# Attention with four score tiles in a row and a group's values in one run: eight weight slots, half of the scalings on GpSimd, four heads of Wo split early

## The chip, the cores and the metric

One core of one Trainium2 chip. The metric is the device time of one execution in microseconds, the median of the runs shown.

## What is computed

The kernel computes a chain of four residual layers on x (64 sequences, 32 tokens, 512 wide). The first, the one that the change touches, is attention with a paged cache:

```python
q, k, v = x @ Wq.T, x @ Wk.T, x @ Wv.T          # 32 query heads, 8 key heads, 128 wide
q, k = rope(rmsnorm(q)), rope(rmsnorm(k))
kc, vc = k_cache[block_table], v_cache[block_table]   # 16 pages of 32 keys per sequence
k_all, v_all = concat(kc, k), concat(vc, v)           # 544 keys, 4 query heads share one key head
scores = where(valid, q @ k_all.T * SCALE, -1e30)
o = softmax(scores) @ v_all
x = x + o @ Wo.T
...
```

The other three are small mixtures of low-rank layers.

## The kernel before

**Stages.** `project` multiplies x by the query, key and value weights and spills the result to device memory (up to about 549 us of the profile), `attend` does the attention of all 64 sequences (to 1664 us), `finish` multiplies by Wo and does the other layers. They share one program without a barrier between them.

**Attention.** The unit of work n is one tile of scores: one sequence b (n // 8), four key heads at once (a, one for each 32 columns of TensorE), and one of the four query heads that share each of them. Its result is 128 rows by 544 keys. Two rounds of four key heads (hh) make a batch b: 8 units, or two groups m of REP = 4 units. For each unit:

- TensorE scores it (`score`, line 948) into one of two score banks, 8 matmuls, which the trace shows as 16 records. It waits until DVE has read the tile that was in this bank two units before (`masked`).
- DVE adds the mask, takes the row maximum and writes the tile to a slot of `probs` (`lower_scores`, line 895).
- ACT takes the exponential and the row sums (`weigh`, line 853); DVE inverts the sums (`invert`, line 902); ACT scales the tile by them (`normalise`, line 859).
- DVE transposes the tile in blocks of 32x32 into `p_t` (`turn`, line 909).

For each group m, TensorE then multiplies the four transposed tiles by the values (`weigh_values`, line 968), 17 slots of keys by 4 row tiles, 68 matmuls, 136 records. Before, they are issued in two halves u = 2m and 2m + 1 of 9 and 8 slots. When both groups of a batch are summed, ACT copies the four output banks (`evacuate`, line 865).

**What sets the order.** Each engine has its own list, written out by these loops. TensorE goes by periods t of two units:

```python
for t in range(PERIODS + SUM_LAG):
    if t < PERIODS:
        score(2 * t)
        score(2 * t + 1)
    if t >= SUM_LAG:
        weigh_values(t - SUM_LAG)
```

with SUM_LAG = 3. ACT and DVE go by periods as well: ACT scales the two tiles of the period before, then weighs this period's; DVE masks this period's two, then transposes the two before.

**Loads.** SyncE issues all transfers of the attention, in the order of batches b: 16 pages of keys and values (line 127, after a table load at line 123), the batch's own keys (131) and own values (791), its queries (134), in batches 2 to 7 four heads of Wo (813), and the store of the outputs of batch b-3 (796). `kv` has BUFS = 3 buffers, so SyncE first waits for the semaphore `summed`:

```python
for b in range(B):
    if b >= BUFS:
        sp.wait_ge(summed, 4 * (b - BUFS + 1))
```

Batch b's first score waits for its pages, its own keys and its queries (`pages_in`, `q_in`).

**Wo.** The product with Wo uses each weight as an upper and a lower part. GpSimd makes both for the first HI_EARLY = 8 heads during the attention (lines 836, 840); the other heads are split in `finish` in pieces of two heads: ACT makes the upper part (1249), DVE (1363) or, for three pieces, GpSimd (1176) the lower. The outputs are split as well (`o_hi` line 176, `o_lo` line 183); TensorE's product is at lines 1405 to 1407.

Of the kernel before, what the change touches and what calls it, by code (L numbers as in the profile page):

```python
# [16 lines left out]
B, S, D = 64, 32, 512  # L17
# [22 lines left out]
HI_EARLY = 8  # L40
# [693 lines left out]
def attend(nc, block, sem, projected, copied, seq_f, pages, in_page_i, key_index, q_t, kv, pages_in, q_in, wo_early,  # L734
# [6 lines left out]
    PERIODS = UNITS // 2  # L741
# [3 lines left out]
    SLOTS_P = 4  # L745
    SUM_LAG = 3

    with ExitStack() as ctx:
# [27 lines left out]
        normed = sem("weights_normed")  # L776
# [11 lines left out]
        def _(sp):  # L788
# [27 lines left out]
            sp.wait_ge(summed, 4 * (B - 2))  # L816
            load_late(sp)
            store(B - 3)
            sp.wait_ge(summed, 4 * (B - 1))
# [10 lines left out]
        def _(pool):  # L830
            pool.wait_ge(projected, NSL * NT)

            def upper_weights(h):
# [7 lines left out]

            for h in range(HI_EARLY):
                pool.wait_ge(normed, (SPLIT_FROM + h) * HK + 2)
                upper_weights(h)
                pool.wait_ge(normed, (SPLIT_FROM + h) * HK + 6)
                lower_weights(h)

        @block.scalar
        def _(act):
# [6 lines left out]
            def normalise(n):  # L856
                i = n % SLOTS_P
                act.wait_ge(inverted, n + 1)
                nc.scalar.activation(probs[:, i], probs[:, i], ACT.Copy, scale=inv_sum[:, i:i + 1]).then_inc(normed, 1)  # L859

            def evacuate(b):
                act.wait_ge(summed, 4 * b + 4)
# [21 lines left out]
        def _(dve):  # L884
# [19 lines left out]
            def turn(n):  # L904
                m, r = n // REP, n % REP
                dve.wait_ge(normed, n + 1)
                if r == 0:
                    at_least(dve, summed, 2 * (m - 1))
# [7 lines left out]
            for t in range(PERIODS):  # L916
                lower_scores(2 * t)
                lower_scores(2 * t + 1)
                if t >= 1:
                    turn(2 * t - 2)  # L920
                invert(2 * t)
                if t >= 1:
                    turn(2 * t - 1)
                invert(2 * t + 1)
                if t % 4 == 0 and t // 4 + 1 < B:
                    build_mask(t // 4 + 1)
            turn(UNITS - 2)
# [608 lines left out]
```

## Time and profile before

| what | value |
| --- | --- |
| median of three runs | 2237.34 us (2234.61 to 2237.67) |
| profiled execution, its own time | 2232.94 us |
| its span | 2231.1 us |
| mean granted TensorE clock | 0.996 |
| PE / PEld / DVE / ACT / POOL busy | 97% / 74% / 66% / 63% / 10% |
| DMA, hardware queue | 485.62 MB, 67.0% of 16 engines' span |
| score matmuls, line 948 | 8192 records |
| values matmuls, line 968 | 17408 records |

A record's length on TensorE is modelled and records overlap, so lengths of stages are best read from start to start. Times are microseconds from the span's start. "idle before" names what ended a wait; "issue" means that the profile shows nothing that was waited for. SyncE's rows (SPq) are the issue of transfers, not the transfers themselves.

### The profile page before, as it was taken

To read this page: it belongs to the slowest core of one execution; us is meant where nothing else is said; L and a number is where in the kernel's file an instruction comes from. 1 tells how busy PE (TensorE), PEld (TensorE's weight loads), DVE (VectorE), ACT (ScalarE), POOL (GpSimd) and SP (SyncE) were. 2 spreads that over 40 slices of the span, in tenths; PEclk is the share of its full clock that TensorE was granted. 3 is DMA by queue.
4 is the path that set the end of the run, shared out by engine and by line. 5 is a ranking of instruction groups with operands and counts; after the bars stand their busy time and mean duration, and the time that the engine had idled before them with its cause. 6 is when DMAs were issued, how large, how long until landed. Compare 5 with 4: busy or idle time off the path is not lost.

```text
span 2231.1 us, 77515 instructions
## 1 busy us (share of the span) xinstructions
PE 2164.1 (97%) x30576; PEld 1652.3 (74%) x30576; DVE 1472.3 (66%) x3643; ACT 1397.4 (63%) x4178; POOL 213.5 (10%) x195
## 2 busy tenths in 40 slices
PE   8999999999899999999999999999999999999998
PEld 6888888887666767767667676676777888888886
DVE  5799999993666766767666676667766433433433
ACT  4788888884677777777777777777773222222221
POOL 4211111110000110000000000000014101101101
PEclk9999999999999999999999999999999999999998
DMA  5344444448899999999999999999973323333331
GB/s 192 100 121 124 116 113 113 131 96 273 312 358 340 328 325 320 326 327 318 328 311 327 318 327 328 310 316 329 337 256 121 107 89 101 106 97 101 108 94 44
DMA packets 355296, 490.21 MB, mean 220 GB/s; under 512 B 59025, under 2 KB 191377, under 8 KB 352018
## 3 DMA queue, kind: packets, MB, share of 16 engines
q1 hardware_dynamic: 354962, 485.62, 67.0%
q8 instruction: 226, 3.70, 0.7%
q14 instruction: 108, 0.88, 0.1%
HBM read 397.37 MB, written 88.08 MB: 218 GB/s over the span
## 4 chain that ended last, share of the span: by engine, by line
PE 71%; DVE 16%; issue 7%; SPq 3%; DMA 2%; ACT 1%; DVEq 0%; ACTq 0%
PE o_bank L968 24%; PE s_bank L948 22%; DVE q_t L653 5%; PE proj L1405 5%; PE proj L1407 5%; PE proj L1406 5%; DVE part_s L644 4%; DVE q_t L669 4%; SPq L127 1%; PE wide L1447 1%; PE wide L1448 1%; PE slim L1436 1%; PE wide L1452 1%; PE turn L1426 1%; PE acc L723 1%
## 5 line engine op out<-in xcount | busy, mean ns | idle before, releaser
L968 PEld LDWEIGHTS o_bank<-p_t,kv 32*128 32x128 f32 x17408 | 518.7, 186 | 129.8 <-issue 126.0
L895 DVE CUSTOM_DVE_ANT_0 probs<-s_bank,mask 128x544 f32<-128x544 f32 x512 | 370.6, 724 | 353.2 <-PE s_bank L948 353.1
L968 PE MATMUL o_bank<-p_t,kv 32*128 32x128 f32 x17408 | 572.9, 277 | 20.0 <-issue 17.4
L948 PE MATMUL s_bank<-kv,q_t 128*32 128x288 f32 (+1 forms) x8192 | 533.4, 397 | 22.8 <-issue 20.7
L853 ACT ACTIVATE probs<-probs,neg_max 128x544 f32<-128x544 f32 x512 | 382.9, 751 | 257.8 <-DVE neg_max L895 245.8
L948 PEld LDWEIGHTS s_bank<-kv,q_t 128*32 128x32 f32 x8192 | 249.7, 110 | 217.0 <-issue 33.5
L909 DVE STREAM_TRANSPOSE p_t<-probs 128x544 f32<-128x544 f32 x512 | 365.2, 731 | 0.4 <-ACT probs L859 0.4
L859 ACT ACTIVATE probs<-probs,inv_sum 128x544 f32<-128x544 f32 x512 | 356.6, 750 | 0.0
L724 PE MATMUL acc<-w_hi,x_lo 128*128 128x512 f32 x764 | 301.8, 395 | 0.0
L723 PE MATMUL acc<-w_lo,x_hi 128*128 128x512 f32 x764 | 301.8, 395 | 0.0
L722 PE MATMUL acc<-w_hi,x_hi 128*128 128x512 f32 x764 | 301.8, 395 | 0.0
L548 ACT ACTIVATE squares<-acc 128x128 f32<-128x128 f32 x640 | 168.6, 278 | 70.2 <-PE acc L724 70.2
L539 ACT ACTIVATE normed<-acc,kv 128x128 f32<-128x128 f32 x640 | 185.2, 392 | 0.1
L722 PEld LDWEIGHTS acc<-w_hi,x_hi 128*128 128x128 f32 x764 | 143.3, 188 | 35.1
L724 PEld LDWEIGHTS acc<-w_hi,x_lo 128*128 128x128 f32 x764 | 143.2, 187 | 35.1
L723 PEld LDWEIGHTS acc<-w_lo,x_hi 128*128 128x128 f32 x764 | 143.2, 187 | 35.1
L1405 PE MATMUL proj<-hi_late,o_hi 128*128 128x512 f32 x384 | 157.1, 409 | 3.4 <-DVE o_lo L183 3.4
L1216 ACT ACTIVATE low_t<-turn 128x128 fp32r<-128x128 f32 (+1 forms) x48 | 15.0, 313 | 231.8 <-PE turn L1456 231.8
L1407 PE MATMUL proj<-hi_late,o_lo 128*128 128x512 f32 x384 | 151.4, 394 | 0.0
L1406 PE MATMUL proj<-lo_early,o_hi 128*128 128x512 f32 x384 | 151.0, 393 | 0.0
L548 ACT ACTIVATION_READ_ACCUMULATOR squares<-acc 128x1 f32 x640 | 132.5, 207 | 0.0
L653 DVE TENSOR_TENSOR q_t<-normed,kv 128x256 f32<-128x256 f32 x320 | 131.5, 452 | 0.0
(141 smaller groups left out, 2334.7 us busy)
## 6 DMA issues: line engine op xcount, KB each, us to landing
kv<-in_kv_pages SPq DMA_DIRECT2D x1024, 256.0 KB, 4.5
q_spill<-wo_early SPq DMA_DIRECT2D x512, 64.0 KB, 1.8
q_t<-q_spill SPq DMA_DIRECT2D x64, 512.0 KB, 5.8
o_spill<-o_t SPq DMA_DIRECT2D x64, 512.0 KB, 6.5
raw<-o_spill SPq DMA_DIRECT2D x64, 512.0 KB, 3.5
kv<-in_w_qkv SPq DMA_DIRECT2D x11, 1024.0 KB, 5.7
v_spill<-wo_early SPq DMA_DIRECT2D x8, 1024.0 KB, 7.8
k_spill<-wo_early SPq DMA_DIRECT2D x128, 64.0 KB, 1.8
```

Of the source, the lines that this page charges most:

```text
L548: last = nc.scalar.activation(squares[:, i, h], acc_of(n)[:, h * HD:(h + 1) * HD], ACT.Square, accum_out=sumsq[:, i, h:h + 1])
L722: pe.matmul(bank, x_hi[:, c, toks], w_hi[:, s % 2, c], start=c == 0, stop=False)
L723: pe.matmul(bank, x_hi[:, c, toks], w_lo[:, s % 2, c], start=False, stop=False)
L724: last = pe.matmul(bank, x_lo[:, c, toks], w_hi[:, s % 2, c], start=False, stop=c == DC - 1)
L853: nc.scalar.activation(probs[:, i], probs[:, i], ACT.Exp, scale=-1.0, bias=neg_max[:, i:i + 1], accum_out=row_sum[:, i:i + 1]).then_inc(we ...
L859: nc.scalar.activation(probs[:, i], probs[:, i], ACT.Copy, scale=inv_sum[:, i:i + 1]).then_inc(normed, 1)
L895: nc.vector.tensor_tensor_reduce(out=probs[:, i], in0=s_run(n), in1=mask[:, b % 2], scale=-SCALE, scalar=3.0e38, op0=ALU.add, op1=ALU.min, ...
L909: nc.vector.transpose(p_t[:, m % 2, :, r], probs[:, n % SLOTS_P].rearrange("p (c e) -> p c e", e=S))\
L948: last = pe.matmul(s_banks[n % 2][rows, columns].rearrange("p (s t) -> p s t", t=PSIZE), q_t[:, b % 2, g, r * S:(r + 1) * S], kv[:, buf, s ...
L968: last = pe.matmul(o_banks[a][:, hh * ROWS:(hh + 1) * ROWS], kv[rows, buf, c, VALUES + hh * HD:VALUES + (hh + 1) * HD], p_t[rows, m % 2, c ...
L1405: pe.matmul(projs[par][:, :], o_hi[:, c % 2, i], upper, start=h == 0, stop=False)
L1407: last = pe.matmul(projs[par][:, :], o_lo[:, c % 2, i], upper, start=False, stop=h == HQ - 1)
```

## The change

It does five things. TensorE scores the four tiles of a group in a row and then does all 136 records of values of a group as one run; SUM_LAG becomes 2, counted in groups. `probs` and its sums get eight slots instead of four. The even units are scaled by GpSimd, the odd ones by ACT, each with a semaphore of its own. DVE masks the four tiles of a group first and transposes the four of the group before afterwards. HI_EARLY becomes 4, so four more heads (two pieces) are split in `finish`. `summed` now counts 2 for a batch instead of 4.

```diff
-HI_EARLY = 8
+HI_EARLY = 4
...
-    SLOTS_P = 4
-    SUM_LAG = 3
+    SLOTS_P = 2 * REP
+    SUM_LAG = 2
...
-                    sp.wait_ge(summed, 4 * (b - BUFS + 1))
+                    sp.wait_ge(summed, 2 * (b - BUFS + 1))
...
+            def normalise(n):
+                i = n % SLOTS_P
+                pool.wait_ge(inverted, n + 1)
+                nc.gpsimd.tensor_scalar(probs[:, i], probs[:, i], inv_sum[:, i:i + 1], None, ALU.mult).then_inc(normed[0], 1)
...
-            for h in range(HI_EARLY):
-                pool.wait_ge(normed, (SPLIT_FROM + h) * HK + 2)
-                upper_weights(h)
-                pool.wait_ge(normed, (SPLIT_FROM + h) * HK + 6)
-                lower_weights(h)
+            for n in range(0, UNITS, 2):
+                normalise(n)
+                h, step = n // HK - SPLIT_FROM, n % HK
+                if 0 <= h < HI_EARLY:
+                    if step == 2:
+                        upper_weights(h)
+                    if step == 6:
+                        lower_weights(h)
...
-                act.wait_ge(summed, 4 * b + 4)
+                act.wait_ge(summed, 2 * b + 2)
...
-            for t in range(PERIODS):
-                done = t - SUM_LAG
-                if done > 0 and done % 4 == 0:
-                    evacuate(done // 4 - 1)
-                if t > 0:
-                    normalise(2 * t - 2)
-                    normalise(2 * t - 1)
-                weigh(2 * t)
-                weigh(2 * t + 1)
-            normalise(UNITS - 2)
-            normalise(UNITS - 1)
+            for m in range(GROUPS):
+                done = m - SUM_LAG
+                if done > 0 and done % 2 == 0:
+                    evacuate(done // 2 - 1)
+                for r in range(REP):
+                    weigh(REP * m + r)
+                normalise(REP * m + 1)
+                normalise(REP * m + 3)
+            evacuate(B - 2)
...
-            for t in range(PERIODS):
-                lower_scores(2 * t)
-                lower_scores(2 * t + 1)
-                if t >= 1:
-                    turn(2 * t - 2)
-                invert(2 * t)
-                if t >= 1:
-                    turn(2 * t - 1)
-                invert(2 * t + 1)
...
+            for m in range(GROUPS):
+                first = REP * m
+                lower_scores(first)
+                lower_scores(first + 1)
+                lower_scores(first + 2)
+                invert(first)
+                lower_scores(first + 3)
+                invert(first + 1)
+                for r in range(REP):
+                    if m > 0:
+                        turn(first - REP + r)
+                    if r < 2:
+                        invert(first + 2 + r)
...
-            for t in range(PERIODS + SUM_LAG):
-                if t < PERIODS:
-                    score(2 * t)
-                    score(2 * t + 1)
-                if t >= SUM_LAG:
-                    weigh_values(t - SUM_LAG)
+            for m in range(GROUPS + SUM_LAG):
+                if m < GROUPS:
+                    for r in range(REP):
+                        score(REP * m + r)
+                if m >= SUM_LAG:
+                    weigh_values(m - SUM_LAG)
```

How the lists of two engines stand before and after, in the middle of the attention. A score tile is two rows, 288 and 256 keys for four key heads each; `o_bank` rows are values. TensorE before, one group:

```order
L968 MATMUL o_bank<-p_t,kv 128x128 x32
L948 MATMUL s_bank<-kv,q_t 32x288 x4
L948 MATMUL s_bank<-kv,q_t 32x256 x4
L948 MATMUL s_bank<-kv,q_t 32x288 x4
L948 MATMUL s_bank<-kv,q_t 32x256 x4
L968 MATMUL o_bank<-p_t,kv 128x128 x36
L948 MATMUL s_bank<-kv,q_t 32x288 x4
L948 MATMUL s_bank<-kv,q_t 32x256 x4
L948 MATMUL s_bank<-kv,q_t 32x288 x4
L948 MATMUL s_bank<-kv,q_t 32x256 x4
L968 MATMUL o_bank<-p_t,kv 128x128 x32
```

TensorE after, one group:

```order
L976 MATMUL o_bank<-p_t,kv 128x128 x68
L958 MATMUL s_bank<-kv,q_t 32x288 x4
L958 MATMUL s_bank<-kv,q_t 32x256 x4
L958 MATMUL s_bank<-kv,q_t 32x288 x4
L958 MATMUL s_bank<-kv,q_t 32x256 x4
L958 MATMUL s_bank<-kv,q_t 32x288 x4
L958 MATMUL s_bank<-kv,q_t 32x256 x4
L958 MATMUL s_bank<-kv,q_t 32x288 x4
L958 MATMUL s_bank<-kv,q_t 32x256 x4
L976 MATMUL o_bank<-p_t,kv 128x128 x68
```

The two runs of values (36 and 32 matmuls) between pairs of tiles have become one run of 68 behind four tiles. DVE before, one period (line 895 masks a tile, 909 transposes, 902 inverts):

```order
L895 ISA probs,neg_max<-s_bank,mask 128x544
L895 ISA neg_max 128x1
L895 ISA probs,neg_max<-s_bank,mask 128x544
L895 ISA neg_max 128x1
L909 STREAM_TRANSPOSE p_t<-probs 128x17x32
L902 RECIPROCAL inv_sum<-row_sum 128x1
L909 STREAM_TRANSPOSE p_t<-probs 128x17x32
L902 RECIPROCAL inv_sum<-row_sum 128x1
```

DVE after, from the third mask of one group on (line 901 masks, 915 transposes, 908 inverts):

```order
L901 ISA neg_max 128x1
L908 RECIPROCAL inv_sum<-row_sum 128x1
L901 ISA probs,neg_max<-s_bank,mask 128x544
L901 ISA neg_max 128x1
L908 RECIPROCAL inv_sum<-row_sum 128x1
L915 STREAM_TRANSPOSE p_t<-probs 128x17x32
L908 RECIPROCAL inv_sum<-row_sum 128x1
L915 STREAM_TRANSPOSE p_t<-probs 128x17x32
L908 RECIPROCAL inv_sum<-row_sum 128x1
L915 STREAM_TRANSPOSE p_t<-probs 128x17x32 x2
```

All four transposes of a group now stand behind the four masks of the next one; before, two stood behind each pair.

## Rows read from the trace of the kernel before

**Rows 1.** The page, part 1: busy us (share of the span) and instructions

```profile
PE 2164.1 (97%) x30576; PEld 1652.3 (74%) x30576; DVE 1472.3 (66%) x3643; ACT 1397.4 (63%) x4178; POOL 213.5 (10%) x195
```

**Rows 2.** Stretch of attention: us, PE, PEld, DVE, ACT, POOL busy (records), PEclk, DMA, GB/s

```profile
605.00:1639.00 1034.00, 1003.56 (x24004) 720.02 (x24000) 707.88 (x1980) 771.06 (x1680) 15.14 (x16) 1.00 0.97 327
```

**Rows 3.** TensorE's timeline: start, us, engine, line, record, count

```profile
1498.35 2.07 PE L968 MATMUL o_bank<-p_t,kv 32*128 32x128 f32 x64
...
1505.05 2.04 PE L948 MATMUL s_bank<-kv,q_t 128*32 128x288 f32 x32
1507.02 2.07 PE L968 MATMUL o_bank<-p_t,kv 32*128 32x128 f32 x64
1509.02 2.04 PE L948 MATMUL s_bank<-kv,q_t 128*32 128x288 f32 x32
1510.99 2.29 PE L968 MATMUL o_bank<-p_t,kv 32*128 32x128 f32 x72
1513.21 2.04 PE L948 MATMUL s_bank<-kv,q_t 128*32 128x288 f32 x32
...
1521.37 2.04 PE L948 MATMUL s_bank<-kv,q_t 128*32 128x288 f32 x32
```

**Rows 4.** TensorE's timeline, a gap inside a run of values

```profile
1123.65 0.93 PE L968 MATMUL o_bank<-p_t,kv 32*128 32x128 f32 x18 [1.53 <-issue]
```

**Rows 5.** Timelines of TensorE and SyncE around the first score of a batch

```profile
1531.49 2.07 PE L968 MATMUL o_bank<-p_t,kv 32*128 32x128 f32 x64
...
1548.90 1.13 SPq L134 DMA_DIRECT2D q_t<-q_spill  x1
...
1555.39 0.91 PE L948 MATMUL s_bank<-kv,q_t 128*32 128x288 f32 x12 [1.32 <-issue]
```

**Rows 6.** SyncE's timeline, the loads of the batch scored at 1521.37

```profile
1502.97 8.82 SPq L127 DMA_DIRECT2D kv<-in_kv_pages  x16
...
1515.23 0.42 SPq L134 DMA_DIRECT2D q_t<-q_spill  x1
```

**Rows 7.** Line 134, the query load: time to landing, min/median/max

```profile
DMA to landing us min/median/max: 4.4/5.8/10.8
```

**Rows 8.** Start of the attention, timelines of TensorE and DVE

```profile
549.46 4.13 PE L948 MATMUL s_bank<-kv,q_t 128*32 128x288 f32 x64
...
550.77 0.72 DVE L895 CUSTOM_DVE_ANT_0 probs<-s_bank,mask 128x544 f32<-128x544 f32 x1 [0.52 <-PE s_bank L948]
```

**Rows 9.** SyncE's timeline, the loads of batch 2

```profile
567.15 8.94 SPq L127 DMA_DIRECT2D kv<-in_kv_pages  x16
...
579.94 0.40 SPq L134 DMA_DIRECT2D q_t<-q_spill  x1
```

**Rows 10.** GpSimd and DVE side by side in the attention

```profile
716.51 0.61 POOL L836 CAST hi_early<-wo_early 128x512 fp32r<-128x512 f32 x1 [229.20 <-ACT probs L859]
726.12 1.28 POOL L840 TENSOR_TENSOR lo_early<-wo_early,hi_early 128x512 fp32r<-128x512 f32 x1 [8.99 <-ACT probs L859]
...
726.29 0.74 DVE L909 STREAM_TRANSPOSE p_t<-probs 128x544 f32<-128x544 f32 x1
```

**Rows 11.** After the attention, timelines of DVE, GpSimd and TensorE

```profile
1666.63 2.36 DVE L1363 TENSOR_TENSOR lo_early<-wo_early,hi_late 128x1024 fp32r<-128x1024 f32 x2 [2.16 <-ACT hi_late L1249]
1669.47 6.23 DVE L1363 TENSOR_TENSOR lo_early<-wo_early,hi_late 128x1024 fp32r<-128x1024 f32 x2 [0.48 <-ACT hi_late L1249]
...
1668.63 5.98 POOL L1176 TENSOR_TENSOR lo_early<-wo_early,hi_late 128x1024 fp32r<-128x1024 f32 x2 [2.57 <-ACT hi_late L1249]
...
1679.05 0.50 PE L1405 MATMUL proj<-hi_late,o_hi 128*128 128x512 f32 x1 [3.42 <-DVE o_lo L183]
```

**Rows 12.** Two waits and the clock of their stretch

```profile
565.52 2.07 PE L968 MATMUL o_bank<-p_t,kv 32*128 32x128 f32 x64 [2.14 <-DMA kv<-v_spill]
...
584.55 3.68 PE L948 MATMUL s_bank<-kv,q_t 128*32 128x288 f32 x32 [4.62 <-issue]
...
560.00:600.00 40.00, 32.74 (x760) 22.92 (x756) 22.52 (x64) 23.87 (x54) 0.00 (x0) 0.96 0.84 297
```

More of the change, by code:

```diff
@@ L740, in attend @@
     UNITS = B * HK
[L741 removed]
+    GROUPS = UNITS // REP
     BANK = 512
@@ L815, in _ @@
                     store(b - BUFS)
-            sp.wait_ge(summed, 4 * (B - 2))
+            sp.wait_ge(summed, 2 * (B - 2))
             load_late(sp)
             store(B - 3)
-            sp.wait_ge(summed, 4 * (B - 1))
+            sp.wait_ge(summed, 2 * (B - 1))
             store(B - 2)
@@ L858, in normalise @@
                 act.wait_ge(inverted, n + 1)
-                nc.scalar.activation(probs[:, i], probs[:, i], ACT.Copy, scale=inv_sum[:, i:i + 1]).then_inc(normed, 1)
+                nc.scalar.activation(probs[:, i], probs[:, i], ACT.Copy, scale=inv_sum[:, i:i + 1]).then_inc(normed[1], 1)
             def evacuate(b):
-                act.wait_ge(summed, 4 * b + 4)
+                act.wait_ge(summed, 2 * b + 2)
                 at_least(act, o_stored[b % 2], b // 2 * 16)
@@ L905, in turn @@
                 m, r = n // REP, n % REP
-                dve.wait_ge(normed, n + 1)
+                dve.wait_ge(normed[n % 2], n // 2 + 1)
                 if r == 0:
-                    at_least(dve, summed, 2 * (m - 1))
+                    at_least(dve, summed, m - 1)
                 nc.vector.transpose(p_t[:, m % 2, :, r], probs[:, n % SLOTS_P].rearrange("p (c e) -> p c e", e=S))\
@@ L915, in _ @@
             build_mask(0)
[L916 to L928 removed]
+            for m in range(GROUPS):
[11 more added lines that the diff above has]
+                        invert(first + 2 + r)
+                if m % 2 == 0 and m // 2 + 1 < B:
+                    build_mask(m // 2 + 1)
+            for r in range(REP):
+                turn(UNITS - REP + r)
             for c in range(2):
@@ L951, in score, with weigh_values @@
                 last.then_inc(scored, 1)
-            def weigh_values(u):
-                m, half = u // 2, u % 2
+            def weigh_values(m):
                 b, hh = m // 2, m % 2
                 buf = buf_of(b)
-                if half == 0:
-                    pe.wait_ge(turned, REP * (m + 1))
-                    if m == 0:
-                        pe.wait_ge(copied, NV * NT)
-                elif hh == 0:
-                    pe.wait_ge(v_own_in[buf], 16 * QUAD * (b // BUFS + 1))
-                for c in range(CUT) if half == 0 else range(CUT, SLOTS):
+                pe.wait_ge(turned, REP * (m + 1))
+                if m == 0:
+                    pe.wait_ge(copied, NV * NT)
+                for c in range(SLOTS):
+                    if hh == 0 and c == NPP:
+                        pe.wait_ge(v_own_in[buf], 16 * QUAD * (b // BUFS + 1))
                     for a in range(QUAD):
@@ L972, in weigh_values @@
                 last.then_inc(summed, 1)
-            for t in range(PERIODS + SUM_LAG):
-                if t < PERIODS:
-                    score(2 * t)
-                    score(2 * t + 1)
-                if t >= SUM_LAG:
-                    weigh_values(t - SUM_LAG)
+            for m in range(GROUPS + SUM_LAG):
+                if m < GROUPS:
+                    for r in range(REP):
+                        score(REP * m + r)
+                if m >= SUM_LAG:
+                    weigh_values(m - SUM_LAG)
         return summed, o_out
@@ L1123, in _ @@
             follow_chunk(0, 3)
-            sp.wait_ge(summed, 4 * B)
+            sp.wait_ge(summed, 2 * B)
             for i, ids in enumerate((slot2, slot3)):
@@ L1160, in _ @@
         def _(pool):
-            pool.wait_ge(summed, 4 * B)
+            pool.wait_ge(summed, 2 * B)
             nc.gpsimd.iota(expert_i[:, :], [[1, E]], base=0, channel_multiplier=0).then_inc(expert_set, 1)
```

3 lines of the change are left out of this document (1 added, 2 removed).

## The prediction

> **What bounds the kernel now.** I read the page first, then one view for each question it left. TensorE is busy 97% of the span, DVE 66%, ACT 63% [rows 1], so nothing that DVE, ACT or GpSimd does less of is worth anything by itself. The stage that the change touches, the attention, needs a closer look, so I took its round. The window from the start of batch 3 to that of batch 63 holds 24,004 TensorE records, 60 batches of 128 for scores and 272 for values, in 1034.0 us: 17.23 us a batch, with TensorE busy 1003.56 us of it and DMA at 0.97, 327 GB/s [rows 2]. A stage in which two resources are both near full is bounded by whichever comes late in each round.
>
> The timeline of TensorE gives the same round without stalls. Two tiles are scored in 2.04 us and the values begin 1.97 us after the start of the scores; a half of values takes 1.99 us (64 records) or 2.22 us (72 records) from start to start. That is 8.16 us for a group of four tiles; a batch of two groups runs from 1505.05 to 1521.37, 16.32 us [rows 3]. So of 17.23 us a batch, 0.91 us is stall. The rows show two kinds: a gap marked "issue" inside a run of values, where no semaphore is named (1.53 us) [rows 4], and a gap of 1.32 us before a batch's first score, again marked "issue", which ends 6.5 us after that batch's query load was issued, which is how long such a load takes (median 5.8) [rows 5, 7]. The loads are therefore only just hidden, and the argument turns on them.
>
> **The loop that hides the loads.** Keys and values have three buffers. SyncE may load batch b when the values of batch b-3 are summed. One batch in rows: the last values of batch b-3 run from 1498.35 for 2.07 us, so the buffer is free at R = 1500.42 [rows 3]; the first page is issued at 1502.97, the queries at 1515.23 [rows 6], and they take 5.8 us to land [rows 7], at 1521.0; the batch's first score starts at S = 1521.37. From R to landed queries L is 2.55 + 12.26 + 5.8 = 20.6 us. From R to S TensorE has five periods of two scores and a half of values, 20.95 us. The cover is larger than the load by 0.3 us. In another batch R is 1531.49 + 2.07 = 1533.56 and S is 1555.39: 21.8 us, and TensorE waited [rows 5].
>
> **The change, part by part.**
>
> *Four scores in a row, then both halves of a group's values in one run.* Joining two runs of values removes one switch each way. Eight records more cost 0.22 us (2.29 against 2.07), so 64 would cost 1.76 of their 1.99; the fixed part is about 0.2, and the joined run is 1.99 + 2.22 - 0.2 = 4.01 us. Joining the scores should save as much, but there are two score banks, and the third tile waits until DVE has masked the first. The rows show this case: at the start of the stage four tiles were scored in a row, 4.13 us with DVE's first mask pass at 550.77 (0.72 us) between them, against 2 x 2.04 for two pairs [rows 8]. So the scores take 4.13 - 0.07 = 4.06 us start to start. A group is 8.07 instead of 8.16 us, a batch 16.14 instead of 16.32: the gain is 0.18 us, 11 us over 60 batches, and no more.
>
> *The lag.* This is where I expect the time to go. Before, values half u stands behind the scores of period u + 3, so the last half of batch b-3 is followed by five periods before batch b is scored, 1.25 batches. After, the values of group m stand behind the scores of group m + 2: the last group of batch b-3 (2b-5) stands in iteration 2b-3, and batch b is scored in iteration 2b. Two iterations lie between, exactly one batch. The cover falls from 20.4 us (five quarters of 16.32) to 16.1, the load of 20.6 stays. TensorE is in order, so the values that it could do stand behind the waiting score.
>
> How long a batch then takes: the buffer of batch b is free one batch's work W after S(b-2), and S(b) = S(b-2) + W + L, so a batch takes (W + L)/2 if that is more than W. For W I take 16.14 plus the stalls inside the runs: of the 0.91 us I give 0.5 to them (bounds: 0.1 if they mend with DMA less pressed, 1.0 if all were of this kind), 16.6. For L the bounds are 19.4 and 21.8. The low one is a load into an idle queue: first page at 567.15, queries issued 12.79 us later [rows 9], plus the least landing time of 4.4 [rows 7] and about 2.2 from R to the first page. The high one is the batch above. After the change the previous batch's queries have landed just before the first page is issued, so the queue is emptier than in the typical 20.6; I take 20.3. That gives (16.6 + 20.3)/2 = 18.45 us, 1.22 more than 17.23, and over 60 batches **+73 us**.
>
> Here a page bears on the sum. The Trainium skill, Runtime: NRT & Kernel Launch, section Instruction fetch mechanics, says that instructions come in blocks by DMA and that the fetch is mostly hidden; my reading of the "issue" gaps inside runs [rows 4] speaks against it. By that page W would be 16.14 and the batch 18.2 us, 14 us less in all.
>
> *Half of the scalings on GpSimd, eight slots.* ACT gives up 2 of 4 scalings a group. Its 771.06 us of work are 6.4 us a group of 8.16 [rows 2], hidden behind TensorE, so less of it is worth nothing. GpSimd's own price for 128x544 is in no row; between the cast of 128x512 (0.61 us) and the two-input subtraction (1.28 us) [rows 10] I take the cast's, since it also reads one tensor. Two in 8 us are nothing, and each has until the next group's transposes, about 6 us, since DVE now does all four transposes behind the next group's scores. DVE's own work does not change: 707.88 us over 120 groups, 5.9 of 8.07 us [rows 2]; it holds. ACT's four evacuations stand at the head of a group, before any tile is masked. Zero for all of it; were this cover gone, each microsecond by which the transposed weights come late would be one of W.
>
> *Four heads of Wo instead of eight split early.* Two more pieces of 128x1024 have to be split after the attention. DVE takes 1.2 us for one when undisturbed (2.36 for two), and TensorE already waits 3.42 us there for o_lo, which stands behind DVE's pieces [rows 11]. Between 0 and 6 us; I take +2, as the new piece stands behind that same o_lo. The last batch's evacuation is no longer hidden under scores: +1.
>
> **The sum.** -11 is already in W. 73 + 2 + 1 = +76 us on the profiled execution's own 2232.9 us, 2309. That execution lies 4.4 us under the median of the runs shown (2237.3), so I forecast **2313 us**.
>
> **Rivals.**
>
> *The load becomes short enough* (other side, faster). If L is under W, TensorE is never held at a batch, and the batch takes W: 16.14 + 0.5, 0.59 us less than now, 35 us less in all, 2205 us with the tail's +3. It decides at L = 16.6. For: DMA is the pressed resource, and a queue with fewer things in it lands sooner. Against: even into an idle queue the queries were issued 12.8 us after the first page and their landing took 4.4 at least [rows 7, 9]. If L falls to 17.9 the result is no change. I give faster 0.07, same 0.03.
>
> *The clock falls in the new waits.* A wait of 4.62 us at 584.55 was followed by two scores of 3.68 instead of 2.04 us, and the granted clock of that stretch is 0.96, others 1.00; a wait of 2.14 us at 565.52 left the scores at 2.04 [rows 12]. The forecast wait is 18.45 - 16.6 = 1.9 us a batch. Should waits alternate between none and 3.8, each long one could cost 1.6 us: 30 of them, +50, 2363 us. Chance 0.12.
>
> *DVE and GpSimd hold each other up.* After the attention DVE first needed 2.36 us for two subtractions, and 6.23 us for the next two, when GpSimd had begun its own [rows 11]. If a GpSimd operation held DVE's mask for 1.28 us once in every run of scores, W would be 16.6 + 2.6 = 19.2 and a batch (19.2 + 20.3)/2 = 19.75, +151 + 3, 2391 us; it decides once DVE's mask comes late at all. Against: next to GpSimd's subtraction at 726.12 DVE's transpose began 0.17 us after it and still took 0.74 us, so the two ran together [rows 10]. The Trainium skill, SBUF — State Buffer, section SBUF: two separate sides, says that the two share a port pair as an exclusive lock, held for a whole instruction, against DVE operations of two SBUF inputs or a two-port mode; by that rule only such operations wait. The rows agree. Chance 0.05.
>
> *The change does nothing to the order.* The instruction order printed with the change excludes it.
>
> **The numbers.** The forecast's own mechanism has 0.73. Its bounds: a batch of (16.2 + 19.4)/2 = 17.8 gives +34 + 3, 2274 us; (17.1 + 21.8)/2 = 19.45 gives +133 + 9, 2379. The clock's case lies inside that. 2268 to 2368 us leaves out the faster case, the unchanged one, the locked one and the top of the load's range, 2 in 10. A measurement of this kernel tells 0.2% (4.5 us) from no change. Faster 0.07, same 0.03, slower 0.90: the three slow cases together.
>
> **What would show it.** Right: in the timeline TensorE idle 1 to 3 us before the first score of nearly every batch, ended by q_t or marked "issue", and none of that size elsewhere; four scores of 4.1 us, values runs of about 4.1; batches of 18 to 19 us; DMA under 0.97 and about 300 GB/s; GpSimd's scalings near 0.65 us. Wrong: batches of 16.6 us with no wait for queries; or scores runs well over 4.13 us, which would put the loss on DVE and the masks; or transposes over 0.75 us; or a granted clock well below 1.00 in the middle slices.

## The result, and the profile after

| | us |
| --- | --- |
| before, in the same job | 2237.51 (2234.61 to 2246.55) |
| changed | 2339.07 (2336.83 to 2345.33) |
| ratio | 1.0456, 95% interval 1.043 to 1.0482 |
| span of the profiled execution, before and changed | 2231.1 and 2335.4 |
| forecast | 2313, range 2268 to 2368 |

The change costs 4.6%. The page of the changed kernel, part 1, which answers to [rows 1]:

```profile
PE 2179.7 (93%) x30576; PEld 1653.7 (71%) x30576; DVE 1477.0 (63%) x3645; ACT 1259.0 (54%) x3924; POOL 622.9 (27%) x443
```

No engine has become the bound: TensorE's busy time grew by 15.6 us, the span by 104.3. The rest is idle TensorE. The same 60 batches as in [rows 2], from the start of batch 3 to that of batch 63 (us, then PE, PEld, DVE, ACT, POOL busy, the granted clock, DMA, GB/s):

```profile
603.40:1739.00 1135.60, 1019.32 (x24001) 723.06 (x24000) 710.07 (x1980) 640.12 (x1440) 399.99 (x248) 0.97 0.87 298
```

The stretch takes 1135.6 us instead of 1034.0, 18.93 us a batch instead of 17.23: 101.6 of the 104.3 us of span are here. DVE does the same work, ACT less. DMA fell from 0.97 to 0.87: over the whole span its packets took the same time as before (63.9% of 2335.4 us, 1492 us, against 1495), so it is idle more often and not slower. The granted clock fell from 1.00 to 0.97.

TensorE's timeline, three batches of it (start, us, engine, line, record, count, idle before):

```profile
1183.79 4.24 PE L976 MATMUL o_bank<-p_t,kv 32*128 32x128 f32 x136
1190.11 5.56 PE L958 MATMUL s_bank<-kv,q_t 128*32 128x288 f32 x64 [2.08 <-issue]
1195.60 4.08 PE L976 MATMUL o_bank<-p_t,kv 32*128 32x128 f32 x136
...
1203.67 4.08 PE L976 MATMUL o_bank<-p_t,kv 32*128 32x128 f32 x136
1207.68 4.72 PE L958 MATMUL s_bank<-kv,q_t 128*32 128x288 f32 x64
1212.33 4.08 PE L976 MATMUL o_bank<-p_t,kv 32*128 32x128 f32 x136
1216.34 4.13 PE L958 MATMUL s_bank<-kv,q_t 128*32 128x288 f32 x64
1220.40 4.08 PE L976 MATMUL o_bank<-p_t,kv 32*128 32x128 f32 x136
1227.91 5.79 PE L958 MATMUL s_bank<-kv,q_t 128*32 128x288 f32 x64 [3.44 <-issue]
1233.63 2.62 PE L976 MATMUL o_bank<-p_t,kv 32*128 32x128 f32 x84
```

SyncE's timeline, the loads of the batch whose first score is at 1227.91, and the first page of the next:

```profile
1208.95 10.62 SPq L127 DMA_DIRECT2D kv<-in_kv_pages  x16
1219.62 0.42 SPq L131 DMA_DIRECT2D kv<-k_spill  x1
1220.09 1.81 SPq L791 DMA_DIRECT2D kv<-v_spill  x4
1221.95 0.42 SPq L134 DMA_DIRECT2D q_t<-q_spill  x1
...
1226.29 9.60 SPq L127 DMA_DIRECT2D kv<-in_kv_pages  x16
```

Line 134 in the changed kernel, time to landing, as in [rows 7]:

```profile
DMA to landing us min/median/max: 4.6/5.8/9.8
```

Read together: the values that free the buffer run from 1203.67 for 4.08 us, so R is 1207.75. The first page is issued 1.20 us later, the queries at 1221.95, and with 5.8 us to land they are there at 1227.75; the score starts at 1227.91. L is 20.0 us. Between R and that score TensorE had the batch of 1207.68 and 1216.34, which ended at 1224.48, and then nothing to do for 3.44 us. This is the mechanism of the forecast. The stretch holds 38 such waits among 60 batches, 74.9 us together (here and below counted from start to start, which gives 0.07 us more for each than the idle time in the rows).

What the sum of the prediction left out, and only a rival had, stands in the same rows: after each long wait the four scores took 5.79 and 5.56 us instead of 4.13. The clock around the later one (columns as above):

```profile
1219.00:1227.00 8.00, 5.47 (x164) 4.37 (x156) 4.54 (x14) 5.34 (x14) 3.27 (x2) 1.00 0.99 336
1227.00:1234.00 7.00, 6.09 (x76) 4.43 (x80) 2.40 (x8) 2.09 (x5) 0.26 (x1) 0.76 0.91 307
1234.00:1242.00 8.00, 7.95 (x208) 5.68 (x204) 6.03 (x18) 4.54 (x11) 3.10 (x3) 1.00 0.99 321
```

The mean of 0.76 over 7 us is 3.4 us at the lower level, 1.2 GHz, and the rest at 2.4. The stretch has 20 such falls, the same stretch before none. 17 of them begin within 1.4 us of a batch's first score that had waited: behind 10 of the 13 waits over 2.5 us, 7 of the 16 between 1 and 2.5, none of the 9 shorter ones.

The groups of DVE, GpSimd and ACT (line, engine, operation, count, busy us, mean ns, idle before):

```profile
L901 DVE CUSTOM_DVE_ANT_0 probs<-s_bank,mask 128x544 f32<-128x544 f32 x512 | 370.9, 725 | 454.8 <-PE s_bank L958 443.7
...
L836 POOL TENSOR_SCALAR probs<-probs,inv_sum 128x544 f32<-128x544 f32 x256 | 419.3, 1647 | 846.1 <-DVE inv_sum L908 845.5
...
L915 DVE STREAM_TRANSPOSE p_t<-probs 128x544 f32<-128x544 f32 x512 | 348.7, 718 | 0.5 <-PE o_bank L976 0.5
...
L867 ACT ACTIVATE probs<-probs,inv_sum 128x544 f32<-128x544 f32 x256 | 185.6, 743 | 0.0
```

A scaling on GpSimd takes 1.65 us, on ACT 0.74. DVE's masks and transposes have their old lengths (0.72 and 0.73 on average before), so GpSimd's scalings did not hold them up.

### The profile page after: what moved, and what is told of

It reads as the page before. It is cut to its first block, busy times and chain, and to the rows that moved or that the text cites. A ratio compares the mean times of both kernels' runs of the same rounds, so it can differ in the third digit from the quotient of the medians.

```text
span 2335.4 us, 77499 instructions
## 1 busy us (share of the span) xinstructions
PE 2179.7 (93%) x30576; PEld 1653.7 (71%) x30576; DVE 1477.0 (63%) x3645; ACT 1259.0 (54%) x3924; POOL 622.9 (27%) x443
## 3 DMA queue, kind: packets, MB, share of 16 engines
q1 hardware_dynamic: 354962, 485.62, 63.9%
## 4 chain that ended last, share of the span: by engine, by line
PE 76%; SPq 7%; issue 6%; DMA 6%; DVE 4%; ACT 1%; DVEq 0%; ACTq 0%
PE o_bank L976 17%; PE s_bank L958 15%; PE acc L723 8%; PE acc L724 8%; PE acc L722 8%; SPq L127 5%; DMA kv<-k_spill 5%; PE proj L1413 5%; PE proj L1415 4%; PE proj L1414 4%; DVE probs L901 2%; PE wide L1455 1%; PE slim L1444 1%; PE wide L1460 1%; PE wide L1456 1%
## 5 line engine op out<-in xcount | busy, mean ns | idle before, releaser
L958 PE MATMUL s_bank<-kv,q_t 128*32 128x256 f32 (+1 forms) x8192 | 565.5, 418 | 93.0 <-issue 83.0
L836 POOL TENSOR_SCALAR probs<-probs,inv_sum 128x544 f32<-128x544 f32 x256 | 419.3, 1647 | 846.1 <-DVE inv_sum L908 845.5
L976 PEld LDWEIGHTS o_bank<-p_t,kv 32*128 32x128 f32 x17408 | 508.9, 187 | 94.5 <-issue 94.3
L976 PE MATMUL o_bank<-p_t,kv 32*128 32x128 f32 x17408 | 539.9, 274 | 36.9 <-issue 35.8
L958 PEld LDWEIGHTS s_bank<-kv,q_t 128*32 128x32 f32 x8192 | 263.7, 115 | 353.6 <-issue 126.1
L915 DVE STREAM_TRANSPOSE p_t<-probs 128x544 f32<-128x544 f32 x512 | 348.7, 718 | 0.5 <-PE o_bank L976 0.5
L1413 PE MATMUL proj<-hi_late,o_hi 128*128 128x512 f32 x448 | 183.1, 409 | 3.8 <-DVE lo_early L1371 3.3
L867 ACT ACTIVATE probs<-probs,inv_sum 128x544 f32<-128x544 f32 x256 | 185.6, 743 | 0.0
L1415 PE MATMUL proj<-hi_late,o_lo 128*128 128x512 f32 x448 | 175.8, 392 | 0.0
L1193 POOL TENSOR_TENSOR up_lo<-up,up_hi 128x512 fp32r<-128x512 f32 x32 | 41.0, 1282 | 416.1 <-ACT up_hi L1230 416.1
```

The lines of the kernel that those rows point to most:

```text
L836: nc.gpsimd.tensor_scalar(probs[:, i], probs[:, i], inv_sum[:, i:i + 1], None, ALU.mult).then_inc(normed[0], 1)
L915: nc.vector.transpose(p_t[:, m % 2, :, r], probs[:, n % SLOTS_P].rearrange("p (c e) -> p c e", e=S))\
L958: last = pe.matmul(s_banks[n % 2][rows, columns].rearrange("p (s t) -> p s t", t=PSIZE), q_t[:, b % 2, g, r * S:(r + 1) * S], kv[:, buf, s ...
L976: last = pe.matmul(o_banks[a][:, hh * ROWS:(hh + 1) * ROWS], kv[rows, buf, c, VALUES + hh * HD:VALUES + (hh + 1) * HD], p_t[rows, m % 2, c ...
L1413: pe.matmul(projs[par][:, :], o_hi[:, c % 2, i], upper, start=h == 0, stop=False)
L1415: last = pe.matmul(projs[par][:, :], o_lo[:, c % 2, i], upper, start=False, stop=h == HQ - 1)
```

## The experiments

All times are medians; the ratio is to the kernel before in the same job, whose median was 2238.17 in the first job (A), 2237.55 in the second (B) and 2236.04 in the third (C).

| run | what it is | us | ratio (95%) | us a batch |
| --- | --- | --- | --- | --- |
| before_wait1 (A) | before, load held to a cover of one batch | 2325.25 | 1.0408 (1.0355 to 1.0461) | 18.80 |
| before_12pages (A) | before, 12 pages | 2197.22 | 0.9826 (0.9779 to 0.9872) | 16.67 |
| after_12pages (A) | change, 12 pages | 2238.96 | 0.9996 (0.9961 to 1.003) | 17.55 |
| after_qfirst (A) | change, queries loaded early | 2260.05 | 1.0105 (1.0059 to 1.0151) | 17.58 |
| after_halves_12pages (B) | change, 12 pages, TensorE's old order | 2226.98 | 0.9954 (0.9934 to 0.9974) | 17.18 |
| after_halves (B) | change, TensorE's old order | 2329.56 | 1.0407 (1.0385 to 1.0429) | 18.87 |
| before_qfirst (B) | before, queries loaded early | 2217.31 | 0.9917 (0.9881 to 0.9954) | 16.99 |
| after_act_scales (B) | change, all scalings on ACT | 2332.63 | 1.0428 (1.0389 to 1.0467) | 18.81 |
| before_12pages_wait1 (C) | before, 12 pages, cover of one batch | 2209.09 | 0.987 (0.984 to 0.99) | 16.86 |
| before_hi4 (C) | before, four heads of Wo early | 2235.23 | 0.9994 (0.9971 to 1.0016) | 17.29 |
| after_halves_qfirst (C) | change, old order, queries early | 2240.07 | 1.0012 (0.9993 to 1.0031) | 17.37 |
| after_filled (C) | change, TensorE kept busy while it waits | 2320.89 | 1.0371 (1.0343 to 1.0399) | 18.70 |

### Is it the cover?

**before_wait1** gives the kernel before the change's cover and nothing else of it: SyncE waits for one more count of `summed`, a quarter of a batch.

```diff
-                    sp.wait_ge(summed, 4 * (b - BUFS + 1))
+                    sp.wait_ge(summed, 4 * (b - BUFS + 1) + 1)
```

> The kernel before with one number changed: SyncE waits for one half of values more (4(b-2)+1 instead of 4(b-2)) before it loads a batch. That takes one of the five periods of cover away and leaves every engine's order, the scalings and the slots as they were. Theory of the cover: the batch goes from 17.2 us to (W + L)/2 with W = 17.2 to 17.8 and L = 19.5 (as the changed kernel's trace has it), 18.4 to 18.7 us, so +70 to +90 us, 2305 to 2330 us, with 1 to 3 us of idle before most batches' first scores and clock falls. Rival (the loss comes from four tiles in a row, from GpSimd or from DVE's new order): no change, 2237 us within 0.5%.

2325.25 us. One number in one wait reproduces 87 us of the change's 102. Its stretch of 60 batches and one of its batch starts:

```profile
601.70:1729.40 1127.70, 1031.12 (x24002) 735.33 (x24000) 707.90 (x1980) 772.21 (x1680) 15.14 (x16) 0.97 0.88 301
```

```profile
1184.86 2.29 PE L968 MATMUL o_bank<-p_t,kv 32*128 32x128 f32 x72
1191.13 2.68 PE L948 MATMUL s_bank<-kv,q_t 128*32 128x288 f32 x32 [3.98 <-issue]
1193.74 3.03 PE L968 MATMUL o_bank<-p_t,kv 32*128 32x128 f32 x64
```

Clock, DMA share and GB/s are those of the changed kernel, with 40 waits before first scores (88.1 us) and the same 20 falls of the clock. So most of the loss has nothing to do with four tiles in a row, slots or GpSimd.

**before_12pages and after_12pages** take the load away instead: from batch 3 on only 12 of 16 pages are loaded, with the same amount of arithmetic. The other four keep what the buffer held, so a quarter of the cached keys and values is not the sequence's own; these kernels serve to time the load and nothing else.

```diff
-                for i in range(NPP):
+                for i in range(NPP if b < BUFS else 12):
...
-                    pe.wait_ge(pages_in[buf], 16 * (NPP + 1) * (b // BUFS + 1))
+                    pe.wait_ge(pages_in[buf], 16 * (NPP + 1 + 13 * (b // BUFS)))
```

> The kernel before, but from batch 3 on only 12 of the 16 pages are loaded; the rest of the buffer keeps old pages, so a quarter of the cached keys and values is not the sequence's own. L becomes 2 to 3 us shorter and DMA works about 20% less. Cover theory: only the small waits go, and the stalls inside runs shrink if they come from a pressed DMA: 16.5 to 17.0 us a batch, 2195 to 2225 us. Rival (TensorE alone bounds it and its stalls have nothing to do with DMA): 2237 us.

> The changed kernel with 12 of 16 pages loaded from batch 3 on, as in the run beside it. Cover theory: L falls from 19.5 to about 17, near W, so the waits before the batches and the clock falls go and the batch takes 16.4 to 17.1 us instead of 18.9: 2200 to 2235 us, level with the kernel before with 12 pages within 1% and up to 11 us faster from the switches saved. Rival (masks, GpSimd or DVE's order hold it): it stays above 2300 us.

before_12pages gave 2197.22 us, as expected. after_12pages gave 2238.96: 100 us faster than the change with all pages, but 42 us above before_12pages, where I expected them within 1%, and 4 us over the range. Their stretches, in this order:

```profile
601.90:1602.20 1000.30, 990.96 (x24004) 710.29 (x24000) 707.94 (x1981) 772.15 (x1681) 15.13 (x16) 1.00 0.83 276
```

```profile
603.10:1656.00 1052.90, 996.40 (x24006) 703.37 (x24000) 710.02 (x1980) 639.56 (x1440) 399.77 (x248) 0.99 0.79 261
```

TensorE is busy 5 us longer, the stretch is 53 us longer (the profiled execution of after_12pages took 2252.28 us, 13 over its median); the difference is idle time. 17.2 us of it are waits before first scores, though L is only 16.7 us here: W is 17.4 in this run, above the 16.1 of clean rows, and a batch that TensorE reaches late frees its buffer late. Six falls of the clock, each 3.4 us at half speed, cost 10 us, and most of the rest is gaps inside the runs of values: steps over 250 ns from one record to the next add up to 29.8 us, against 8.6 in before_12pages. The first theory, that the cover is all, had failed at this point.

### What else is in it?

**after_halves_12pages and after_halves** put TensorE's order of before back into the change (two tiles, half of the values), with the cover, the slots and GpSimd left as changed.

```diff
-            def weigh_values(m):
+            def weigh_values(m, half):
...
-                for c in range(SLOTS):
+                for c in range(CUT) if half == 0 else range(CUT, SLOTS):
...
-                    for r in range(REP):
-                        score(REP * m + r)
-                if m >= SUM_LAG:
-                    weigh_values(m - SUM_LAG)
+                for half in range(2):
+                    if m < GROUPS:
+                        score(REP * m + 2 * half)
+                        score(REP * m + 2 * half + 1)
+                    if m >= SUM_LAG:
+                        weigh_values(m - SUM_LAG, half)
```

> The changed kernel with 12 of 16 pages, and TensorE's order alone put back: two tiles, a half of the values, two tiles, the other half. Lag, slots, GpSimd, DVE's order stay changed. With 12 pages the load hardly holds, and the changed kernel still stood 42 us above the kernel before with 12 pages (2239 against 2197). Theory of the burst: a run of 136 records of values uses 272 instructions in 4 us, and TensorE's instructions cannot be fetched at that rate, so gaps marked issue grow with the length of the run; put back, the gaps inside runs fall from about 96 to 40 us and the time to 2195 to 2210 us. Rival (masks, GpSimd's scaling of 1.65 us or DVE's order cause the rest): it stays at 2239 us.

> The same order of TensorE with all 16 pages. The cover is one batch still, so by the theory of the cover it stays slow, as the kernel before with one half less of cover did (2325 us); the burst's share is hidden partly in the waits before the batches: 2315 to 2332 us, 10 to 20 us under the changed kernel. Rival (the grouping is the main cause): under 2270 us.

after_halves_12pages: 2226.98, a miss; only 12 of the 42 us came back, the clock's falls among them (6 became 1). after_halves: 2329.56, as expected, 10 us under the change. TensorE's grouping, which clean rows make 0.18 us a batch faster, is in the whole kernel 10 us slower.

**after_act_scales** gives all scalings back to ACT, with eight slots and the new order.

```diff
...
-                normalise(REP * m + 1)
-                normalise(REP * m + 3)
+                for r in range(REP):
+                    normalise(REP * m + r)
```

> The changed kernel with all scalings on ACT again, GpSimd doing only the four heads of Wo. ACT has room (54% busy) and the transposes come late after the scalings: no change, 2339 us within 0.4%. If GpSimd and DVE did hold each other up, it would be faster by more.

2332.63 us, 0.3% under the change, and its interval overlaps the change's: moving half of the scalings to GpSimd gains nothing, and a cost of some 6 us is possible but not shown, although each takes 1.65 us.

**before_12pages_wait1** asks whether the cover also explains what is left between before_12pages and after_halves_12pages, 30 us. It has the edits of before_12pages and before_wait1 together.

> The kernel before with 12 of 16 pages loaded from batch 3 on (its output leaves the other four pages' new keys and values out), and SyncE held until a quarter of the next batch's values has been multiplied: the cover is one batch, as in the change, but TensorE's order stays that of before. The same loads without the hold took 2197 us, the change with them 2239, and the change with TensorE's old order 2227. If the one-batch cover is what is left between 2197 and 2227, this run gives 2213 to 2228 us, with 10 to 20 us of waits before first scores. If what is left comes from the slots, the scalings on GpSimd or the order of DVE and ACT, it stays at 2195 to 2203.

2209.09 us, a few us below the range. The cover gives 12 of those 30 us, with 35 short waits before first scores, 21.9 us together. The other 18 us belong to what after_halves_12pages has besides it: slots, the order of DVE and ACT, GpSimd, Wo. The trace shows where the time is, not why. The runs of values of after_halves_12pages take 26.7 us more in all than here (490.4 against 463.7), its scores 3.8 more, and its waits before first scores about 11 less. Of the 26.7 us, 9.7 are in steps over 250 ns; the other 17 are small delays spread over the runs. Their cause stays open.

### The clock

**after_filled** keeps TensorE busy in the wait. Pages and own keys land 1.9 us before the queries (mean, 1.5 to 2.9), so between the two waits of a batch's first score I put eight matmuls whose result is overwritten.

```diff
...
                     pe.wait_ge(pages_in[buf], 16 * (NPP + 1) * (b // BUFS + 1))
+                    if b >= BUFS:
+                        fill(n)
                     pe.wait_ge(q_in[b % 2], 16 * (b // 2 + 1))
```

> The change with eight extra matmuls (one tile of scores, about 1.0 us, of the batch's own keys with themselves, into the score bank that the real tile then overwrites) between the wait for a batch's pages and the wait for its queries, from batch 3 on. They lie in time in which TensorE waited anyway, as long as the load is longer than the work (19.5 us against 16.1 + 2 x 1.0 + the stalls). If the falls of the granted clock after the long waits cost what I read (20 falls, some 34 us of TensorE's time, half of which ends in the batch's cycle), there are fewer than 8 falls between batches 3 and 63 and the time is 2315 to 2330 us. If the falls don't depend on the waits or cost nothing, about 20 stay and the time is 2337 to 2345. If the added work lengthens the cycle, over 2345.

2320.89 us, 18 us faster than the change with 1.0 us a batch more work. Its stretch, and one batch start in it (line 952 is the extra work, 972 the scores, 990 the values):

```profile
604.80:1726.70 1121.90, 1057.29 (x24965) 729.19 (x24961) 709.75 (x1980) 639.39 (x1442) 399.45 (x248) 1.00 0.88 302
```

```profile
1179.78 2.08 PE L990 MATMUL o_bank<-p_t,kv 32*128 32x128 f32 x68
1182.12 1.12 PE L952 MATMUL s_bank<-kv 128*32 128x288 f32 x16 [0.27 <-DMA kv<-k_spill]
1183.62 4.28 PE L972 MATMUL s_bank<-kv,q_t 128*32 128x288 f32 x64 [0.38 <-DMA q_t<-q_spill]
1187.83 4.24 PE L990 MATMUL o_bank<-p_t,kv 32*128 32x128 f32 x136
```

The clock is 1.00, two falls are left of 20, no wait before a first score is over 1.8 us, and the scores behind them take 4.28 us instead of 5.6. DMA and GB/s hardly moved: the load is still the bound, but W fell from 17.83 to 17.39 us. So the falls of the clock depend on the long waits, and they cost some 13 to 18 us of the whole (an estimate: 0.44 us of W, by half, over 60 batches gives 13, the two medians differ by 18).

### The load's last part

**after_qfirst and before_qfirst** issue the query load before the wait for the buffer. Queries have two buffers of their own, and the batch that used this one has been scored by then.

```diff
+                if b >= 2:
+                    sp.wait_ge(scored, (b - 1) * HK)
+                    load_queries(sp, b)
                 if b >= BUFS:
                     sp.wait_ge(summed, 2 * (b - BUFS + 1))
...
-                if b >= 2:
-                    sp.wait_ge(scored, (b - 1) * HK)
-                    load_queries(sp, b)
```

(In before_qfirst the wait is for `4 * (b - BUFS + 1)`.)

> The changed kernel, full work, but SyncE issues batch b's query load before it waits for the buffer, not behind the pages (its own buffer has been free since batch b-2 was scored). The last landing is then that of the own keys behind the pages: L = 1.2 + 14.4 + about 1.5 = 17.1 us instead of 19.5. Cover theory: the batch takes (17.2 + 17.1)/2, about 17.2 us instead of 18.9, and most clock falls go: 2225 to 2260 us. Rival (the bytes moved bound it, not the order of the loads): no change, 2339 us within 1%.

> The kernel before with each query load issued ahead of the wait for the buffer. The load becomes 1.5 to 2.5 us shorter than its cover, so the waits of 12 us in all before the batches' first scores go, the gaps inside runs stay: 2220 to 2232 us. If the waits marked issue before a batch were instruction fetches too, nothing changes: 2238 us.

after_qfirst gave 2260.05 us, at the upper end of what was expected and 79 us off the change: with the queries out of the chain, 27.6 us of waits before first scores are left of 74.9. SyncE's order, and the wait that is now last on TensorE:

```profile
1149.80 3.22 PE L958 MATMUL s_bank<-kv,q_t 128*32 128x288 f32 x48
...
1166.53 4.16 PE L958 MATMUL s_bank<-kv,q_t 128*32 128x288 f32 x64 [1.33 <-DMA kv<-k_spill]
```

```profile
1150.14 9.18 SPq L127 DMA_DIRECT2D kv<-in_kv_pages  x16
1159.38 1.21 SPq L131 DMA_DIRECT2D kv<-k_spill  x1
...
1162.96 0.44 SPq L134 DMA_DIRECT2D q_t<-q_spill  x1
```

The queries issued at 1162.96 are those of the next batch; what TensorE waits for at 1166.53 is the batch's own keys, behind 16 pages. before_qfirst gave 2217.31 us, a little under the expected range. Its stretch:

```profile
601.30:1620.90 1019.60, 1001.97 (x24006) 718.17 (x24006) 707.93 (x1980) 772.41 (x1682) 15.13 (x16) 1.00 0.96 333
```

17.23 us a batch became 16.99, and 12.2 us of waits before first scores became 2.1. This edit to the old kernel beats both kernels, by 0.8% and 5.2%.

**after_halves_qfirst** puts the old order and the early queries into the change together.

> The change with TensorE's order put back to two tiles and half a group's values, and the query load issued ahead of the wait for the buffer. The early queries alone gave 2260 us, the old order alone 10 us off the change and 12 off the change with 12 pages. If the two gains add up, 2245 to 2252 us, still above before (2237.5), since L falls only to where the own keys and pages land. If they overlap, 2255 to 2262.

2240.07 us, level with before; the two gains add up to 99 us where 89 were expected. All that the change then still has of its own (slots, GpSimd, DVE's order, the shorter lag) is worth 23 us more than before_qfirst takes. The shorter lag is large enough to account for it, though no run separates it: the trace has 38 waits before first scores, 29 us together, against 2.1 in before_qfirst, since pages and own keys still land only 17.5 us after the free buffer, and clean work in the old order covers 16.3 (32.64 for two batches less the shortest W, 16.39).

### Wo

**before_hi4** is the kernel before with one number changed.

```diff
-HI_EARLY = 8
+HI_EARLY = 4
```

> The kernel before with four heads of Wo split early instead of eight, nothing else. The prediction's +2 us for this part, with bounds of 0 and 6: 2238 to 2243 us expected, with TensorE's wait for o_lo at the head of the product with Wo longer than 3.4 us. A rival, from the changed kernel's trace, where the time from the last values to the end was 0.5 us shorter than before: within 1 us of 2237.5.

2235.23 us, 0.8 under before in the same job, no change: the rival's answer. The changed kernel's timeline of TensorE after the attention, against the 3.42 us of [rows 11], shows why:

```profile
1773.09 0.50 PE L1413 MATMUL proj<-hi_late,o_hi 128*128 128x512 f32 x1 [0.41 <-DVE lo_early L1371]
...
1776.58 0.47 PE L1413 MATMUL proj<-hi_late,o_hi 128*128 128x512 f32 x1 [0.48 <-POOL lo_early L1184]
...
1780.92 0.50 PE L1413 MATMUL proj<-hi_late,o_hi 128*128 128x512 f32 x1 [1.36 <-DVE lo_early L1371]
...
1785.49 0.47 PE L1413 MATMUL proj<-hi_late,o_hi 128*128 128x512 f32 x1 [1.54 <-DVE lo_early L1371]
```

The one wait for o_lo is gone, and four for the lower parts of Wo's late pieces stand in its place: 3.8 us for 3.4. The trace of before_hi4 has the same four waits, 3.9 us together.

## Why the prediction was right, and where its sum was short

**The direction and its cause** were right: the cover fell to one batch, the load did not, and TensorE idles before the first score. before_wait1 shows this by itself.

**The cycle.** The prediction put a batch at (W + L)/2 with W = 16.6 and L = 20.3, 18.45 us, +73 over 60 batches. The trace gives 18.93 and +101.6. Means over the batches:

| term | predicted | measured | us a batch |
| --- | --- | --- | --- |
| L, from the free buffer to landed queries | 20.3 | 19.49 | -0.4 |
| W, from a batch's first score to the buffer it waits for | 16.6 | 17.83 | +0.6 |
| from landed queries to the first score | 0 | 0.71 | +0.35 |

The step that failed is W: "16.14 plus the stalls inside the runs", with 0.5 for them and 1.0 as the bound. The 16.14 is right: the shortest W in the trace is 16.22. The stalls are 1.6 us. Some 0.5 of it is the clock, and the rest gaps inside runs, which mended little when DMA was less pressed (W is still 17.4 in after_12pages). L came out lower since the first page now goes out 1.3 us after the free buffer on average (2.3 in the same stretch of before, 2.55 in the batch that I read). SyncE's last issue of the batch before now always lies at least 1.0 us behind when the buffer comes free; in before it was not done in 14 of 60 batches. The third term was missing from the sum: (W + L)/2 assumes that TensorE is never late, but load and work take turns, and in 22 of 60 batches the queries lay there first. Three errors, of which one had the other sign, left the sum 28.6 us short; with the measured terms it is 19.0 a batch.

**Grouping.** Scores four in a row take 4.05 to 4.08 us from start to start (predicted 4.06) and the shortest run of values 4.01 (predicted 4.01). But "the gain is 11 us" is a statement on clean rounds. From its first record's start to its last one's end the median run of values is clean, 4.08 us, but the mean is 4.47. Most of the difference lies in the run just before a batch's first score, mean 4.72: it holds 27 of the 35 steps over 250 ns. after_halves, without the grouping, has 15.6 us of such steps where the change has 41.2, and is 10 us faster. The third tile does wait for DVE's mask as read from [rows 8]: the steps between tiles are 0.94, 1.18 and 0.94 us.

**Instruction fetch.** The prediction's reading of the gaps marked "issue" inside runs [rows 4] stands against the Trainium skill, Runtime: NRT & Kernel Launch, section Instruction fetch mechanics, by which crossing a block is mostly hidden; that would have made W 16.14. The trace carries the reading: the long gaps recur at nearly the same place of every 256 instructions, and in the stretch of before 42 gaps over 250 ns that are no batch start, 31.7 us together, end at a median of 1.39 us (8 in 10 within 1.26 to 1.54) after the end of a packet of the instruction queue. By the page the blocks are of 256 instructions, and here the trace agrees. "Mostly" holds too (188 packets, 42 gaps); hidden for good it is not, and this is 3% of the stretch.

**GpSimd** was taken at the cast's price, 0.61 us; it is 1.65, above even the two-input subtraction's 1.28 [rows 10]. It was costed at nothing as it is hidden, and that held: after_act_scales differs by 6 us, inside the two intervals. **The rival of the shared port** is out for the attention: DVE's operations kept their lengths there. The changed kernel also repeats the case of [rows 11]: after the attention a DVE subtraction with two SBUF inputs takes 1.22 us alone, and 2.87 and 3.42 us beside GpSimd's subtractions (from 1774.65 on). Both agree with the Trainium skill, SBUF — State Buffer, section SBUF: two separate sides: subtractions of this kind wait, while the mask, with one input in SBUF, and the transpose do not.

**The clock's rival** was not the alternative I made it: it came on top of the forecast. 17 of 38 waits brought a fall, and 3 falls came without one; each costs 1.7 us of TensorE's time (priced at 1.6; one lasted twice as long), 36 in all. About half of that ends in the time, since W enters the cycle by half; the +50 of the prediction had counted each fall whole.

**The rival of a short load** shows in the runs with 12 pages: before_12pages is in that regime. after_12pages reached L = 16.7 and yet W was 17.4, so the point from which it decides is where L is under the work with its stalls, with margin.

**Wo and the end.** The +2 for two more pieces was wrong: before_hi4 is level, and from the last values to the end the changed kernel is 0.5 us shorter. The +1 for the end of the attention was 4.9 (30.2 us from batch 63's start to the last values against 25.3). The larger part is one gap inside values and the slow scores behind it:

```profile
1749.41 0.73 PE L976 MATMUL o_bank<-p_t,kv 32*128 32x128 f32 x17 [2.68 <-issue]
1750.07 5.56 PE L958 MATMUL s_bank<-kv,q_t 128*32 128x288 f32 x64
...
1760.23 8.99 PE L976 MATMUL o_bank<-p_t,kv 32*128 32x128 f32 x272 [0.59 <-ACT o_t L873]
```

Without these 2.7 and 1.5 us it is about 1, as predicted.

## What to carry to other kernels

When a change alters how far the values lag behind the scores, count the work that stands between "the buffer is free" and "the batch that needs it", and compare it with the load from that moment to its last landed byte; with three buffers a quarter of a batch decided 87 us. A load whose destination has its own buffers does not belong behind the wait for another's: moving one DMA gave 0.8% on the tuned kernel. And add the stalls to a clean round from the mean over many rounds: here 16.1 us of clean work was 17.8 on average, and it is the average that enters the cycle.

## What the runs showed of the hardware

- TensorE's granted clock falls from 2.4 to 1.2 GHz after waits of this size: 20 times in a stretch with waits before first scores of up to 3.8 us, twice in one with waits of up to 1.8 us, never in the same stretch of before, whose 14 such waits are 12.2 us together. Each fall in the changed kernel lasted 3.4 us, or twice that, and doubled the time of what ran in it. Work without use, put into the wait, avoided it.
- The gaps from instruction fetch were not the same in all kernels: values runs had 26 steps over 250 ns in before (22.1 us), 35 in the changed kernel (41.2), 13 in before_12pages (8.5) and 7 in before_12pages_wait1 (4.2). In before 25 of the 26 and in the changed kernel 34 of the 35 end 1.2 to 1.6 us after a packet of the instruction queue. They are fewer where DMA is less pressed (after_12pages, at 0.79, has 23, 29.8 us), and at the same DMA share of 0.87 to 0.88 the kernels in TensorE's old order have less of them than the change: before_wait1 14.2 us, after_halves 15.6. Why is not shown.
- `tensor_scalar` on GpSimd over 128x544 with a scalar of each partition took 1.65 us, while the cast of 128x512 took 0.61.
- A DVE subtraction of 128x1024 with both inputs in SBUF took 1.22 us alone and up to 3.42 us beside a GpSimd subtraction, before and after the change; DVE's mask and transpose kept 0.72 us beside GpSimd's scalings.
